# First attention: projections as plain fp32 in two row halves of the array, one double projection a unit

## The reference

```
h = tokens(x)                                   # [16, 255, 64]
h = h + attention0(layernorm(h))                # 8 heads, ranks of 32
h = h + experts0(layernorm(h))                  # 16 experts, best 2 of each token
h = h + attention1(layernorm(h))                # 8 heads of 8, with a position score
h = h + experts1(layernorm(h))                  # 8 experts, best 2
```

```
q = x Q_h ; k = x K_h                # [255, 32] for each of 8 heads
a = softmax(q k^T / sqrt(64))        # [255, 255]
out = sum over heads of (a x) VO_h   # VO_h is [64, 64]
```

## Time and profile before

| | us |
|---|---|
| median of 3 runs | 783.16 |
| the runs | 786.09, 779.23, 783.16 |
| the profiled execution's own time | 777.67 |
| its span, first to last instruction | 775.9 |
| TensorE busy | 651.6 |
| VectorE busy | 606.9 |
| ScalarE busy | 500.7 |
| GpSimd busy | 345.2 |

### The profile page before, as it was taken

How to read it: one execution, slowest core, us unless ns; L and a number is a source line. 1 busy time by engine, 2 the same in 40 slices (tenths; PEclk the granted TensorE clock), 3 DMA queues, 4 the chain that set the end, 5 groups by cost and what they waited for, 6 DMA issues and landing times.

```text
span 775.9 us, 16564 instructions
## 1 busy us (share of the span) xinstructions
PE 651.6 (84%) x5064; PEld 372.0 (48%) x5080; DVE 606.9 (78%) x1670; ACT 500.7 (65%) x1247; POOL 345.2 (44%) x423
## 2 busy tenths in 40 slices
PE   4516898999999997989988888588888888889896
PEld 4504565666666664223333223455555555556332
DVE  5685787988888897778888888848888888867643
ACT  2757776677776773556676667837777777754552
POOL 1017588786877876522223333543444554320000
PEclk9957999999999999999999999889999999996999
DMA  4030000000000000533333222000000000000001
GB/s 105 1 108 1 1 2 1 0 0 0 0 0 0 0 1 1 193 110 111 98 99 103 88 84 83 1 1 1 2 1 0 0 0 0 1 1 1 12 20 24
DMA packets 21750, 24.37 MB, mean 31 GB/s; under 512 B 12358, under 2 KB 12614, under 8 KB 21446
## 3 DMA queue, kind: packets, MB, share of 16 engines
q1 hardware_dynamic: 19463, 23.31, 9.7%
q10 hardware_dynamic: 2239, 0.49, 0.3%
HBM read 22.48 MB, written 1.31 MB: 31 GB/s over the span
## 4 chain that ended last, share of the span: by engine, by line
PE 45%; DVE 21%; ACT 11%; issue 10%; POOL 5%; DMA 2%; DVEq 0%; SPq 0%; ACTq 0%; POOLq 0%
ACT big L910 6%; PE ps L1537 5%; PE ps L634 4%; PE ps L717 3%; PE ps L1559 3%; PE ps L644 3%; DVE big L1034 3%; DVE big L1130 3%; DVE big L1076 2%; PE ps L707 2%; POOL big L1317 2%; PE ps L1786 2%; DVE mid L1143 2%; PE ps L1543 2%; PE ps L734 2%
## 5 line engine op out<-in xcount | busy, mean ns | idle before, releaser
L1317 POOL TENSOR_TENSOR big<-big 128x1024 f32<-128x1024 f32 x64 | 120.5, 1894 | 52.4 <-DVE big L1136 51.8
L910 ACT ACTIVATE big<-ps,big 128x255 f32<-128x255 f32 x256 | 117.9, 487 | 10.2 <-DVE big L1130 9.9
L879 ACT ACTIVATE big<-ps,b1s 128x512 f32<-128x512 f32 x128 | 80.6, 681 | 32.8 <-PE ps L634 32.7
L1130 DVE TENSOR_REDUCE big<-ps 128x4 f32<-128x1020 f32 x64 | 74.6, 1206 | 20.1 <-PE ps L707 20.1
L1143 DVE COPY mid<-ps 128x512 f32<-128x512 f32 x128 | 82.0, 681 | 6.3 <-PE ps L717 2.9
L2044 DVE TENSOR_REDUCE big<-ps 128x4 f32<-128x1020 f32 x64 | 77.9, 1217 | 5.9 <-DVE res L2101 2.5
L717 PE MATMUL ps<-cst,big 128*128 128x128 f32 x512 | 71.5, 280 | 8.8 <-DVE mid L1143 3.1
L902 ACT ACTIVATE big<-ps 128x512 f32<-128x512 f32 x64 | 39.4, 616 | 59.4 <-PE ps L695 33.9
L644 PE MATMUL ps<-big,w2s 128*64 128x512 f32 x256 | 69.6, 622 | 7.2 <-ACT big L879 7.1
L634 PE MATMUL ps<-big,wall 64*128 64x512 f32 x256 | 74.5, 648 | 0.7 <-ACT big L850 0.7
L1904 ACT ACTIVATE big<-ps 128x1024 f32<-128x1024 f32 x64 | 65.8, 1029 | 14.1 <-PE ps L1549 9.6
(11 more groups left out here) (267 smaller groups left out, 1367.8 us busy)
## 6 DMA issues: line engine op xcount, KB each, us to landing
mid<-spread_w SPq DMA_DIRECT2D x128, 128.0 KB, 2.8
mid<-in_split_sel SPq DMA_DIRECT2D x1, 1536.0 KB, 8.7
wall<-in_w SPq DMA_DIRECT2D x1, 1280.0 KB, 7.5
out_tokens<-res SPq DMA_DIRECT2D x16, 56.0 KB, 1.6
cst<-in_consts SPq DMA_DIRECT2D x1, 648.5 KB, 7.1
mid<-in_w_raw SPq DMA_DIRECT2D x1, 620.0 KB, 5.6
w2s<-in_w SPq DMA_DIRECT2D x1, 512.0 KB, 3.3
mid<-in_taps ACTq DMA_DIRECT2D x1, 320.0 KB, 3.9
```

The lines of the kernel that those rows point to most:

```text
L879: last = nc.scalar.activation(hid[e % 2][j], H1(e, j), ACT.Relu, bias=b1s[0][:, 2 * e + j:2 * e + j + 1])
L910: last = nc.scalar.activation(e_sb[r % 4][:, jj, tq, 0:NW], S[:, 2 * (r % 2) + jj, tq, 0:NW], ACT.Exp, scale=-1.0, bias=minus[r % 4][:, jj ...
L1130: nc.vector.tensor_reduce(minus[r % 4], S[:, 2 * a:2 * a + 2, :, 0:NW], AX.X, ALU.min).then_inc(s_mx, 1)
L1317: nc.gpsimd.tensor_tensor(e_sb[r % 4], e_sb[r % 4], bc(inverse[r % 4].unsqueeze(3), [P, 2, 2, 256]), ALU.mult).then_inc(s_A, 1)
```

## The change

Projections of the first attention become plain fp32 matmuls. The columns of a batch are stored as fp32, 64 features on partitions 0 to 63 and the same again on 64 to 127, and so are the weights (`w32`, 1024 columns, in memory that the position scores use later). A "double projection" computes two products at once, one on each 64-row half of the array, each into a bank of its own: M is now banks 7 and 4. Q and K together are one (four matmuls of 256 columns), the two halves of the values are the other (two of 512). Each slot has one double projection instead of two single ones, and it stands ahead of the scores in TensorE's queue. As bank 4 is also the first bank of AT, it waits for the first copy of the previous slot's second round, and the turn of round 2N waits until ScalarE has drained bank 4. The scale of the scores is multiplied into the Q weights by GpSimd in the token phase. The column parts of this stage are gone: each chunk is turned and copied once, the first three chunks by ScalarE, the others by VectorE; chunks 2 and 3 are now normed by VectorE instead of GpSimd. The split weights `w64` keep the 216 columns that the second attention uses, and the raw table is loaded in two transfers.

```diff
-            M = ps[:, 7]
+            M = [ps[:, 7], ps[:, 4]]
+            COLUMN_BANK = (5, 6)
+            BY_ACT = 3
...
+                def project(n, par, d, batch=None):
+
+                    x_of = xs[par] if batch is None else xcol[:, 256 * batch:256 * batch + 256]
+                    if not isinstance(d, int) or d >= 1:
+                        pe.wait_ge(s_out, 2 * d)
+                    if n == QKN:
+                        for w in range(2):
+                            for g in range(2):
+                                half = slice(D * g, D * g + D)
+                                f = (Q0, K0)[w] + P * g
+                                last = nc.tensor.matmul(M[g][:, 256 * w:256 * w + 256], w32[half, f:f + P], x_of[half], start=True, stop=True)
                     else:
-                        c = n - V0N
-                        for m, (kind, start, stop) in enumerate(kinds):
-                            last = nc.tensor.matmul(M, x_of[:, kind, P * c:P * c + P], w64[:, m, V0:V0 + H * D], start=start, stop=stop)
+                        for c in range(2):
+                            half = slice(D * c, D * c + D)
+                            last = nc.tensor.matmul(M[c], x_of[half, P * c:P * c + P], w32[half, V0:V0 + H * D], start=True, stop=True)
                     last.then_inc(s_pr, 1)
...
@@ TensorE, slot @@
+                    ahead = more or par == 0
+                    if ahead:
+                        if g == 0:
+                            pe.wait_ge(s_xs, b + 1)
+                            if not known or b >= 2:
+                                pe.wait_ge(s_add, b - 1)
+                        if not known or N >= 1:
+                            pe.wait_ge(s_at, 4 * N - 1)
+                        project((QKN, VN)[g], 1 - par, N + 2)
                     if more or k < 2 * QUADS - 1:
                         pe.wait_ge(s_E, 2 * N + 2)
                         if g == 1:
                             pe.wait_ge(s_out, 2 * N + 4)
                         scores(k + 1)
-                    if more or par == 0:
-                        if g == 0:
-                            pe.wait_ge(s_xs, b + 1)
-                        project(*first_of(k), FIRST + 2 * N)
                     if known and N == 0:
-                        x_columns(CH - 1)
-                        pe.wait_ge(cols.s_r, CH - 1)
+                        columns_copied(pe, CH - 1)
+                    if ahead:
+                        pe.wait_ge(s_out, 2 * N + 5)
                     turn(2 * k, 2 * N)
                     if g == 1 and (not known or b >= 1):
                         pe.wait_ge(s_O, b)
-                        pe.wait_ge(s_out, 2 * N + (2 if not more and par == 1 else 6))
+                        pe.wait_ge(s_out, 2 * N + 6 if ahead else 4 * B)
                         outputs_turn(1 - par)
...
-                    if more or (par, g) == (0, 0):
-                        if g == 1:
-                            pe.wait_ge(s_xs, b + 2)
-                            if not known or b >= 1:
-                                pe.wait_ge(s_add, b)
-                        project(*second_of(k), FIRST + 2 * N + 1)
                     turn(2 * k + 1, 2 * N + 1)
...
@@ ScalarE, project_out @@
+                def project_out(n, par, d):
+                    act.wait_ge(s_pr, d + 1)
+                    for half in (1, 0):
+                        dst = qk[par][:, half].rearrange("p n q -> p (n q)") if n == QKN else val[par][:, half]
+                        nc.scalar.activation(dst, M[half], ACT.Copy).then_inc(s_out, 1)
...
@@ GpSimd, token phase @@
+                    pool.wait_ge(s_w32, 16)
+                    link(nc.gpsimd.tensor_scalar(w32[:, Q0:K0], w32[:, Q0:K0], -float(D ** -0.5), None, ALU.mult))
...
@@ VectorE and GpSimd, start of the stage @@
+                dve.wait_ge(s_cen, 3)
+                normed(2)
+                normed(3)
                 dve.wait_ge(s_S, 1)
                 for r in range(2):
                     maxima(r)
-                cols.rest(dve, 2)
-                cols.rest(dve, 3)
+                column_out(3)
+                column_out(4)
                 inverses(0, 0)
-                cols.rest(dve, 4)
+                column_out(5)
+                column_out(6)
                 inverses(1, 1)
-                cols.rest(dve, 5)
-                cols.rest(dve, 6)
+                column_out(7)
...
-                cols.low(pool, 0)
-                cols.low(pool, 1)
-                pool.wait_ge(cols.s_lo, 2)
                 fetch(1, 1)
-                for c in range(2, CH):
+                for c in range(4, CH):
                     normed(c)
```

More of the change, by code:

```diff
@@ L180, in tokens @@
             low = spec(4)
-            raw, raw_rest = mid[:, 3328:3328 + W64], mid[:, 4568:4568 + W64]
+            raw, raw_rest = mid[:, 3328:3328 + W64 - W32], mid[:, 4568:4568 + W64 - W32]
             hi, md, lo = (w64[:, s] for s in range(3))
@@ L492, in take_a @@
                 return a
[L493 to L494 removed]
+            qk = [take_a(1024).rearrange("p (g n q) -> p g n q", g=QUADS, n=2) for _ in range(2)]
             e_sb = [take_a(1024).rearrange("p (j t k) -> p j t k", j=2, t=2) for _ in range(4)]
@@ L497, in attention0_and_experts0 @@
             val = [take_a(2 * H * D).rearrange("p (c v) -> p c v", c=2) for _ in range(2)]
-            xs = [take_a(256).bitcast(BF16).rearrange("p (k q) -> p k q", k=2) for _ in range(2)]
+            xs = [take_a(256) for _ in range(2)]
+            xcol = pos_t[:].rearrange("p h c q -> p (h c q)")
             o_sb = [take_a(256) for _ in range(2)]
@@ L516, in attention0_and_experts0 @@
             norm = TileNorm("L0", link, norm_work, 2)
-            QN, KN, V0N, V1N = range(4)
-            FIRST = 5
-            FIRST_BANK = [ps[:, n] for n in (7, 0, 7, 7)]
+            QKN, VN = range(2)
             sq = mid[:, 0:2048].rearrange("p (t d) -> p t d", t=NT)
@@ L528, in attention0_and_experts0, with columns_copied, column @@
             s_b2, s_big_w = sem("a0_output_biases_in"), sem("a0_weights_in")
-            cols = ColumnParts("a0", *columns, (5, 6, 4), [pos_t[:, h].rearrange("p c q -> p (c q)") for h in range(H)])
+            s_turned, s_col_a, s_col_d = (sem(f"a0_{n}") for n in ("rows_turned", "columns_by_act", "columns_by_dve"))
+            def columns_copied(eng, c):
+                if c < BY_ACT:
+                    eng.wait_ge(s_col_a, c + 1)
+                else:
+                    eng.wait_ge(s_col_d, c - BY_ACT + 1)
+            def column(c):
+                return xcol[:, 512 * c:512 * c + 512]
             def sd_at(c):
@@ L676, in x_columns @@
                 def x_columns(c):
-                    if c < 2:
+                    if c < 4:
                         pe.wait_ge(s_x, c + 1)
                     else:
[L680 to L693, removed]
-                            for m, (kind, start, stop) in enumerate(kinds):
-                                last = nc.tensor.matmul(M[:, 256 * g:256 * g + 256], w64[:, m, w:w + P], x_of[:, kind], start=start, stop=stop)
-                    else:
-                        c = n - V0N
-                        for m, (kind, start, stop) in enumerate(kinds):
-                            last = nc.tensor.matmul(M, x_of[:, kind, P * c:P * c + P], w64[:, m, V0:V0 + H * D], start=start, stop=stop)
@@ L924, in slot @@
                     b = 2 * j + par
-                    if (not known or N >= 1) and (more or (par, g) in ((0, 0), (0, 1))):
-                        if g == 1 and (not known or b >= 1):
-                            act.wait_ge(s_PV, 2 * QUADS * b)
-                        if g == 0 and (not known or b >= 1):
-                            act.wait_ge(s_S, 2 * b)
-                        project_out(*second_of(k - 1), FIRST + 2 * N - 1)
                     if more or par == 0:
@@ L1159, in slot @@
                         maxima(2 * k + 3)
-                    if known and N == 0:
-                        cols.rest(dve, CH - 1)
                     if g == 1 and (not known or b >= 1):
@@ L1197, in normed, with column_out @@
                 def normed(c):
-                    dve.wait_ge(s_inv0, 1)
+                    dve.wait_ge(s_inv0, 1 if c < 2 else 2)
                     nc.vector.tensor_tensor(x2[:, TC * c:TC * c + TC], centred_twice(c), sd_at(c), ALU.mult).then_inc(s_x, 1)
+                def column_out(c):
+                    dve.wait_ge(s_turned, c + 1)
+                    nc.vector.tensor_copy(column(c), ps[:, COLUMN_BANK[c % 2]]).then_inc(s_col_d, 1)
                 others = slice(2 * TC, NT)
```

95 lines of the change are left out of this document (32 added, 63 removed).

## The result

The median of the changed kernel is 804.68 us (4 runs, 803.21 to 805.95), that of the kernel before, in runs beside it, 784.62; the ratio is 1.027, 95% interval 1.021 to 1.032. The forecast was 805, +21.9 us; the medians differ by 20.1.

What follows compares the result with a forecast made beforehand. Before, VectorE bounds odd slots, the scores-maxima-exponentials ring even ones; after, a ring through copies and projection. Stage +30.5 us, start -8.6: +21.9 on the 783.16 us median makes 805; own range 797 to 814, 8-in-10 range 787 to 819.

Steps and rivals of the forecast that it cites:

- The copy-to-projection wait, the failing overlap: First attention: projection, then scores, must wait for VectorE's second copies, 0.73 us copy to TensorE; odd slots +1.71, even +0.77.
- The experts' layer as the price of the projection: Projection on TensorE priced at 1.06 us from the experts' hidden layer row, which already includes the tiling mode switches.
- The blocking at L446: Odd slots: VectorE's last norm operation, held up by GpSimd's weighing, stays at 1.44 us, against 0.17 without that neighbour.
- the freed place between the turns: TensorE, where two bf16 projections of 0.82 us each are removed per slot: counted as gaining nothing.
- the drains: ScalarE's two 512-column drains a slot run while scores and maxima run: no cost; 0.60 us each without that cover.
- The start: Start of the first attention: slot 2's maxima at 84.3 against 92.91, -8.6 us, between -4.5 and -11.
- The two corrections ahead of the stage: Before the first attention: VectorE's L330 pair beside a smaller L347, -1.0 us; VectorE's wait for TensorE goes, -0.9.
- the step from the first to the second scores: Start: scores from about 60.0 to about 68.8 us, through maxima, two exponential rounds of 1.9 each and two drains.
- The blocked norms: Start: normed(2) and normed(3) on VectorE beside GpSimd's own cost 0 to 4 us by blocking, taken as +1.3.
- A: Rival: the projection's wait for the copy is already met; pairs stay at 14.03, -11.1 us, 772 us; chance 0.11.
- B: Rival: odd slots' L446 no longer meets GpSimd's weighing, 0.17 for 1.44 us; -17.8, so 787 us; chance 0.10.
- C: Rival: the projection's two halves don't overlap, 0.85 us more for each of 29; +24.7, so 830 us; chance 0.06.

Runs made afterwards that it cites:

- doubled projection: Changed kernel with every matmul of the double projections issued twice in a row: 831.4 us, ratio 1.065 to the kernel before.
- copies-between-maxima version: Changed kernel with the norm behind the second copies and the first copies between VectorE's two maxima: 773.4 us, again 775.5; ratios 0.986 and 0.988 to the kernel before.

## Why the prediction was right

**The copy-to-projection wait, the failing overlap, was right**, and so was its place: odd slots 9.17 us for a forecast of 9.07, even ones 7.47 for 7.44. Term by term: from copies to projection 0.81 us (215.15 to 215.96; forecast 0.73), projection 1.06 (both forms; forecast 1.06), scores to maxima 1.22 and 1.21 (1.21), outputs to what follows 1.02 (1.02), second copies 6.08 us after the maxima (6.07). The pair was 0.13 over the forecast, 0.08 of it the first term. Over 14 pairs that is 1.8 us; the last odd slot, with no projection in it (7.14 us, 2.0 less and not 1.71), and slot 3 (8.95) take back some 0.5, and the stage was +31.7 for +30.5.

**The experts' layer as the price of the projection was right**: the added switches of the array's mode cost no more than that row already held. The blocking at L446 was right too: 1.44 us stayed, and releasing GpSimd later took it away.

**What was counted at nothing:** the freed place between the turns gave nothing back, as forecast; the drains, behind scores and maxima, cost next to nothing (from 86 to 316 us the turn's weight loads wait for them three times, 1.0 us in all); for GpSimd TensorE waits once, 0.5 us.

**The start: -7.5 us for -8.6.** Projection at 54.54 in place of 59.25, as forecast (56.5 less 1.9). The two corrections ahead of the stage came in full: transposes at 52.65 in place of 54.51, 1.86 us for 1.9. Mis-sized was the step from the first to the second scores: I let two rounds of exponentials set it (68.8, less 1.9, plus 1.3: 68.2), measured 69.26. The blocked norms took 3.01 us for two in place of 1.29, 1.7 and not 1.3; but taking them off VectorE left slot 2 where it was (85.31 for 85.42), and in both versions the chain of columns ends the stretch. So this step had the wrong path, the two rounds of exponentials in place of the chain of columns, which the sum puts at nothing. Without the +1.3 the sum has 66.9, and the chain ended 2.4 us later. That the start came out within 1.1 us is partly luck.

**The rivals.** A (the wait met for nothing) would have shown pairs of 14.0: it fell with 16.64 and with the experiment that put the copies ahead of the norm and shortened only the odd slots. B (the blocked norm goes away) did not happen by itself, and was made to happen twice, for 12 us with the norm left in its place and for 15 with the whole norm moved, against the 17.8 it was priced at. C (halves one after another) fell with 1.06 us and with the doubled projection.

**Total.** +24.2 us at slot 30 in the first pair of profiles and +23.4 in the second, +20.1 in the medians, for a forecast of 21.9. So where the change acts, the sum was 1.5 to 2.3 us short (1.2 in the stage, 1.1 at the start), and the medians came out 1.8 under it: the rest of the program, which the change doesn't touch, scatters by about 4 us. That the changed kernel's median is 804.68 for 805 has luck in it, as before's median also moved, from 783.16 to 784.62. The range of 797 to 814 is mis-added at its upper end: its own terms, +7 and +4 on 805, give 816.

## What to carry to other kernels

Before work is moved ahead of the step that closes a ring, ask which buffer it writes and who still reads it: it brings its own length and the reader's delay onto the ring. Here odd slots grew by 1.8 us, 1.08 of it TensorE's wait for the copy, and even slots by 0.8 without such a wait, for a projection that had itself become cheaper (1.06 us in place of two of 0.82). When such a wait is there, the cheap repair is the order on the reader's engine: what is not needed soon goes behind the copy that is waited for. And an order that helps one version can hurt the other, so the two must be tried together.

## What the runs showed of the chip

In some executions TensorE's granted clock fell to its lower level (1.2 of 2.4 GHz) for some 2.5 to 4 us within the stage, behind a wait of TensorE of about 2 us, and in others of the same code it did not. In the first profile of the copies-between-maxima version, the table of stretches around the long odd slot of batch 3:

```profile
...
112.00:118.00 6.00, 5.36 (x45) 2.78 (x44) 4.12 (x8) 5.12 (x19) 5.25 (x13) 1.00 0.01 3
118.00:122.50 4.50, 2.79 (x24) 2.02 (x20) 3.20 (x4) 2.02 (x9) 3.81 (x3) 0.88 0.00 0
122.50:125.00 2.50, 2.50 (x12) 1.79 (x12) 1.65 (x5) 1.93 (x8) 1.40 (x1) 0.53 0.00 0
125.00:130.00 5.00, 5.00 (x49) 3.07 (x45) 3.33 (x11) 1.69 (x5) 3.85 (x4) 1.00 0.00 0
```

The turn had waited 1.71 us for GpSimd's weighing, until 119.75; then the clock was 0.53 from 122.5 to 125, eight instructions of the next turn took 1.97 us in place of 1.09, and the slot took 1.4 us more than in the repeat. The repeat of the same code had the same wait of 1.71 us (until 120.97) and no fall: its eight took 1.09. The same holds for slot 0 of the changed kernel: the turn waits 2.13 us for VectorE's copy in both profiles, the clock stays at 1.00 in the first and is 0.50 from 74 to 77 us in the second, and the slot takes 7.47 and 9.09 us. In slot 0 of the kernel before the turn waits 1.54 us in the first profile, with a clock of 1.00 behind it, and 1.68 in the second, with a clock of 0.52 from 83 to 85 us (7.58 and 9.15 us). In the kernel before with the norm moved, TensorE waited 1.97 us for GpSimd, until 131.09, and the clock was 0.57 from 131 to 135 us. The odd slots of the changed kernel, with 1.1 us of idling in each, brought none. What decides it was not tried.
